# Nine mix products held to the end of the first aggregation, and the small gate matmuls of the last strips placed anew

## What is computed

```python
xn = layernorm(x)
h  = spmm(edges, xn)                                  # first aggregation, A^T applied to xn
S0 = softmax(spmm(edges, h)  @ W0.T + b0)             # first graph layer
S1 = softmax(spmm(edges, [S0, S0]) @ W1.T + b1)       # second graph layer
x  = x + tanh([S0, S1] + h) + mix(xn)                 # mix: linear attention, (q kv) @ wo.T + bo
x  = x + ffn(layernorm(x))                            # top-1 of 8 experts, capacity 489 tokens each
```

## Time and profile before

| | |
|---|---|
| median of 3 runs | 1162.5 us (1161.41 to 1164.13) |
| the profiled execution, first to last instruction (its span) | 1161.9 us |
| TensorE (PE) matmuls, weight loads | 1097.3 us (94%), 701.6 us (60%) |
| VectorE (DVE) | 737.1 us (63%) |
| ScalarE (ACT) | 314.2 us (27%) |
| GpSimd (POOL) | 168.1 us (14%) |
| chain that ended last, by engine | PE 80%, DVE 9%, SPq 3%, issue 3%, ACT 2% |
| its largest lines | L1542 21%, L1691 20%, L1527 11%, L1791 10%, L1779 9%, L1566 2% |
| granted TensorE clock, mean | 0.976 |

### The profile page before, as it was taken

How to read it: one execution, slowest core, us unless ns; L and a number is a source line. 1 busy time by engine, 2 the same in 40 slices (tenths; PEclk the granted TensorE clock), 3 DMA queues, 4 the chain that set the end, 5 groups by cost and what they waited for, 6 DMA issues and landing times.

```text
span 1161.9 us, 14112 instructions
## 1 busy us (share of the span) xinstructions
PE 1097.3 (94%) x4837; PEld 701.6 (60%) x4837; DVE 737.1 (63%) x1681; ACT 314.2 (27%) x1038; POOL 168.1 (14%) x206
## 2 busy tenths in 40 slices
PE   5879999999999999999998999999998799999995
PEld 3446666666666666667793444644447666666664
DVE  8989989998786877777760111116788435554444
ACT  4667767421211222122210111101112211122220
POOL 1112223301010100000000000000234511111111
PEclk9899989999999999999998999999999799999998
DMA  5110111123323223343318998997995584555520
GB/s 168 18 45 13 46 47 46 46 91 121 133 96 133 114 112 121 126 154 136 131 57 323 325 354 292 343 343 275 308 320 213 155 217 117 118 141 136 141 63 7
DMA packets 78871, 178.52 MB, mean 154 GB/s; under 512 B 33567, under 2 KB 62011, under 8 KB 66639
## 3 DMA queue, kind: packets, MB, share of 16 engines
q1 hardware_dynamic: 67550, 126.16, 34.1%
q10 hardware_dynamic: 7120, 43.34, 9.2%
q0 software_dynamic: 4128, 8.08, 2.0%
HBM read 116.23 MB, written 63.77 MB: 155 GB/s over the span
## 4 chain that ended last, share of the span: by engine, by line
PE 80%; DVE 9%; SPq 3%; issue 3%; ACT 2%; DMA 1%; POOLq 0%; POOL 0%; ACTq 0%; DVEq 0%
PE ps L1542 21%; PE ps L1691 20%; PE ps L1527 11%; PE ps L1791 10%; PE ps L1779 9%; PE ps L1566 2%; SPq L465 2%; PE ps L1509 2%; PE ps L1442 1%; PE ps L1495 1%; DVE W L1022 1%; SPq L463 1%; DVE XT L1357 1%; ACT W L746 1%; PE ps L1516 1%
## 5 line engine op out<-in xcount | busy, mean ns | idle before, releaser
L1542 PE MATMUL ps<-RING,XX 128*128 128x512 f32 (+2 forms) x700 | 291.8, 542 | 1.0 <-DVE W L1082 1.0
L1691 PE MATMUL ps<-RING,RY 128*128 128x512 f32 (+4 forms) x750 | 273.7, 523 | 5.8 <-issue 5.8
L1691 PEld LDWEIGHTS ps<-RING,RY 128*128 128x128 f32 x750 | 136.8, 196 | 126.4 <-issue 119.0
L1527 PEld LDWEIGHTS ps<-RING 128*128 128x128 f32 x1250 | 164.5, 193 | 40.8 <-issue 34.1
L774 ACT COPY RING<-ps 128x512 f32<-128x512 f32 (+3 forms) x163 | 91.2, 560 | 312.2 <-PE ps L1527 298.2
L1527 PE MATMUL ps<-RING 128*128 128x128 f32 (+1 forms) x1250 | 171.3, 277 | 0.1
L1542 PEld LDWEIGHTS ps<-RING,XX 128*128 128x128 f32 x700 | 118.5, 191 | 68.8 <-issue 60.7
L1073 DVE TENSOR_TENSOR RING<-iota_n,RY 128x512 f32<-128x512 f32 (+1 forms) x138 | 91.2, 661 | 34.5 <-PE ps L1527 31.8
L1074 DVE TENSOR_TENSOR RING<-iota_n,RY 128x512 f32<-128x512 f32 (+1 forms) x138 | 100.5, 728 | 0.0
L1076 DVE TENSOR_TENSOR RING<-RING,RY 128x512 f32<-128x512 f32 (+1 forms) x138 | 91.1, 660 | 0.0
L900 ACT ACTIVATE RY<-ps,b1T 128x489 f32<-128x489 f32 x64 | 42.9, 670 | 172.2 <-PE ps L1779 172.2
(11 more groups left out here) (258 smaller groups left out, 1295.3 us busy)
## 6 DMA issues: line engine op xcount, KB each, us to landing
RING<-adj_dram SPq DMA_DIRECT2D x60, 1280.0 KB, 6.9
adj_dram<-RING ACTq DMA_DIRECT2D x30, 1280.0 KB, 4.5
rbuf_dram<-W SPq DMA_DIRECT2D x8, 516.0 KB, 5.4
RING<-rbuf_dram SPq DMA_DIRECT2D x8, 516.0 KB, 4.0
xbuf_dram<-W SPq DMA_DIRECT2D x8, 512.0 KB, 3.3
XT<-in_L_ffn_w SPq DMA_DIRECT2D x16, 256.0 KB, 5.1
XT<-in_L_ffn_w SPq DMA_DIRECT2D x4, 1024.0 KB, 8.4
RING<-in_L_ffn_w SPq DMA_DIRECT2D x16, 256.0 KB, 4.9
```

The costliest lines, as they stand in the source:

```text
L1527: last = nc.tensor.matmul(o[:, c:c + w], h[:, 0, i, :], h[:, 1, i, 0:w], start=True, stop=(j != s))
L1542: last = nc.tensor.matmul(ps[:, ACC + dd, 0:w], XN[:, j, dd * H:(dd + 1) * H], at[:, i * w:(i + 1) * w], start=(j == 0), stop=True, skip_g ...
L1691: last = nc.tensor.matmul(o, (Y if l == 0 else S0)[:, j, :], RING[:, slot_of[g % 5], i * across + first:i * across + first + w], start=(j ...
```

## The change

Two separate edits.

**Mix products.** `MIX_AT` ends at tile 15 (iteration 100). Tiles 16 to 24 (`HELD = 16`) come after the loop: 16 and 17 around `hidden_node(23)`, as 22 and 23 did before, and 18 to 24 behind `hidden_node(24)`, ahead of `more_rounds`. They have places of their own in five banks (`HELD_AT`), so none of them waits for a `mixed`; VectorE does the nine `mixed` in a row behind both `hn_out`, each bank's only once all of that bank's products are done. `turns(0, 0)` and `turns(0, 1)`, which use banks 2 and 7, wait for `s_mrd`.

**Last strips.** Strip `kb` keeps `turns(1, ka)` and `logits(ka - 1)` as inserts. `counts(ka - 1)` and `gate_turn(ka)` move from its steps 14 and 22 to steps 4 and 6 of strip `kc`; there `turns(1, kb)` and `logits(ka)` move from steps 4 and 5 to step 13. `counts(ka)` and `gate_turn(kb)` move from step 21 of strip `kc` to behind `turns(1, kc)`. ScalarE does `zout(1, kc)` ahead of `exp8(ka)` and `xtout(kb)`, not behind them.

```diff
--- before.py
+++ after.py
@@ -119,7 +119,8 @@
 for _t in range(NT - 2):
     _k, _i = _t // 4, _t % 4
     HN_AT[NT * _k + 30 + (5 * _i if _k < 5 else _i)] = _t
-MIX_AT = {40 + 4 * _m: _m for _m in range(NT - 3)}
+HELD = 16
+MIX_AT = {40 + 4 * _m: _m for _m in range(HELD)}
 KV_AT, T1_AT, M_AT, FOUND_AT = 33, 37, 39, 60
 
 
@@ -311,7 +312,14 @@
         HNB = 5
         MIXB = 6
         TURN = (2, 7)
-        mix_bank = lambda m: MIXB if m < NT - 2 else ACC + m - (NT - 2)
+        HELD_AT = ((MIXB, 0), (MIXB, D), (KVACC, 0), (KVACC, D), (PROD, 0), (PROD, D), (ACC, 0), (ACC, D), (ACC + 1, 0))
+
+        def mix_out(m):
+            bank, at = HELD_AT[max(m - HELD, 0)]
+            return ps[:, bank, at:at + D]
+
+        def mixes_to_bank(m):
+            return m + 1 if m < HELD else max(n for n in range(HELD, NT) if HELD_AT[n - HELD][0] == HELD_AT[m - HELD][0]) + 1
         XTB = 3
         LGB = 5
         CNB = 6
@@ -879,9 +887,9 @@
             zout(1, kb)
             ex(1, kb)
             tanh(1, kb)
+            zout(1, kc)
             exp8(ka)
             xtout(kb)
-            zout(1, kc)
             ex(1, kc)
             tanh(1, kc)
             xtout(kc)
@@ -1087,9 +1095,9 @@
                 v.tensor_copy(Y[:, t, :], ps[:, HNB, D:D + H]).then_inc(s_hrd, 1)
 
             def mixed(m):
-                dve.wait_ge(s_mixp, m + 1)
+                dve.wait_ge(s_mixp, mixes_to_bank(m))
                 dve.wait_ge(s_bo, m + 1)
-                v.tensor_tensor(X1[:, m, :], X1[:, m, :], ps[:, mix_bank(m), 0:D], ALU.add).then_inc(s_mrd, 1)
+                v.tensor_tensor(X1[:, m, :], X1[:, m, :], mix_out(m), ALU.add).then_inc(s_mrd, 1)
 
             heads = lambda x: x.rearrange("p (h d) -> p h d", d=HD)
             g_v = gvb[:, 0, :].unsqueeze(1).to_broadcast([P, 2, HD])
@@ -1190,11 +1198,10 @@
                 if it - 3 in MIX_AT:
                     mixed(MIX_AT[it - 3])
             strip_out(NS - 1)
-            mixed(NT - 3)
             hn_out(NT - 2)
-            mixed(NT - 2)
             hn_out(NT - 1)
-            mixed(NT - 1)
+            for m in range(HELD, NT):
+                mixed(m)
 
 
             with more_rounds(dve):
@@ -1560,10 +1567,9 @@
 
             def mix(m):
                 pe.wait_ge(s_mv, 1)
-                if m < NT - 2:
-                    ge(pe, s_mrd, m)
+                ge(pe, s_mrd, min(m, HELD))
                 for c in range(2):
-                    last = nc.tensor.matmul(ps[:, mix_bank(m), 0:D], XT[:, c, m * P:(m + 1) * P], M[:, c, :], start=(c == 0), stop=(c == 1))
+                    last = nc.tensor.matmul(mix_out(m), XT[:, c, m * P:(m + 1) * P], M[:, c, :], start=(c == 0), stop=(c == 1))
                 last.then_inc(s_mixp, 1)
 
             turn(0)
@@ -1612,11 +1618,12 @@
                     hidden_node(HN_AT[it])
                 if it in MIX_AT:
                     mix(MIX_AT[it])
-            mix(NT - 3)
+            mix(HELD)
             hidden_node(NT - 2)
-            mix(NT - 2)
+            mix(HELD + 1)
             hidden_node(NT - 1)
-            mix(NT - 1)
+            for m in range(HELD + 2, NT):
+                mix(m)
 
 
             with more_rounds(pe):
@@ -1698,6 +1705,8 @@
             def turns(l, k):
                 b = k % 2
                 pe.wait_ge(s_zev[l], k + 1)
+                if l == 0 and k < 2:
+                    pe.wait_ge(s_mrd, NT)
                 if k >= 2:
                     pe.wait_ge(s_ex[0] if l == 0 else s_nm[1], k - 1)
                 elif l == 1:
@@ -1760,9 +1769,11 @@
                     inserts[23] = [later(gate_turn, k - 1)]
                 strip(1, k, inserts)
             strip(1, ka, {1: [later(logits, ka - 2)], 3: [later(turns, 1, ka - 1)], 15: [later(counts, ka - 2)], 21: [later(gate_turn, ka - 1)]})
-            strip(1, kb, {3: [later(turns, 1, ka)], 4: [later(logits, ka - 1)], 14: [later(counts, ka - 1)], 22: [later(gate_turn, ka)]})
-            strip(1, kc, {4: [later(turns, 1, kb)], 5: [later(logits, ka)], 21: [later(counts, ka), later(gate_turn, kb)]})
+            strip(1, kb, {3: [later(turns, 1, ka)], 4: [later(logits, ka - 1)]})
+            strip(1, kc, {4: [later(counts, ka - 1)], 6: [later(gate_turn, ka)], 13: [later(turns, 1, kb), later(logits, ka)]})
             turns(1, kc)
+            counts(ka)
+            gate_turn(kb)
             logits(kb)
             gate_turn(kc)
             logits(kc)
```

## The result

The median falls from 1162.53 us to 1154.67 (four runs, 1152.17 to 1155.24): -7.9 us by the medians. The ratio over all runs is 0.9926, with a 95% interval of 0.9912 to 0.994; that is -8.6 us, between -10.2 and -7.0. The forecast was 1154.8. Its sum was right, but its term for the clock was not. The two profiles' spans, 1161.9 and 1153.1 us, hide this, since 2.7 us of difference lie ahead of both edits.

The account below looks back on a forecast made before the run. The prediction took TensorE to bound the loop, and VectorE to set the pace in the last strips once the wait goes. Terms -5.2 + 2.5 - 5.0 = -7.7 us, from 1162.5 to 1154.8 us; range 1149.0 to 1159.0.

Parts of the forecast that it names:

- term for the clock: First strip behind the branch: after a 3.1 us idle gap the clock falls as before, no gain; 2.8 us if not.
- the prediction's own last sentence: Wrong if branch time depends more on traffic, the clock stays up, or the queue is deeper than 18 passes.
- Loop: First aggregation's loop, bound by TensorE: six mix products leave it, 0.86 us each, full 5.2 us gained.
- Tail: Loop end to first strip: sequencer lead of 18 passes, branch of 6.0 us, so first strip 2.5 us later.
- The lower bound of 3.1 us: TensorE's branch behind the held products: its shortest time, if it ends when the DMA transfers do.
- The rival of the deep queue: Loop end: all 34 passes fit in TensorE's queue, branch hidden, clock stays up; 1149.7 us, chance 0.10.
- The rival of the short gap: Loop end: branch 4.5 to 5.5 us, gap 1.7 to 2.7, clock stays up; 1151.0 us, chance 0.28.
- Last strips: Strips kb and kc: without the 3.80 us wait, VectorE sets the pace and `biased(kc)` starts 5.0 us earlier.
- edit 2: The last strips' reordering of inserts: forecast gain 5.0 us, bounds 3.3 and 5.8.
- The half gain: Loop bound partly by VectorE's order or stores, or branch fetch 3 to 6 us longer; 1157.4 to 1161.2, chance 0.11.
- the late chunk: Strip kc's first chunk lands late, TensorE stands still and its clock falls; slower, 1164.0 at 14 us, chance 0.03.
- edit 2's moved wait: Last strips: VectorE's order holds `biased(kc)` another 1.7 us or more; 1156.5 to 1158, chance 0.05.

Follow-up runs that it names:

- the first profile: Kernel before, unchanged, profile on which the forecast was built: span 1161.9 us, kernel's median 1162.53 us.
- the other two: Two more profiles of the unchanged kernel before: single times 1164.14 and 1162.86 us.
- held5: Changed kernel with five mix products held (20 to 24), not nine: 1157.68 us, 0.9948 to the kernel before.
- no_branch: Changed kernel without TensorE's fallback and the branch over it: 1150.43 us, 0.9888 to the kernel before.
- after: The changed kernel itself, first profile: median 1154.67 us, 0.9926 to the kernel before.
- before_2: Second profile of the kernel before, nothing changed: single time 1164.14 us.
- after_again: The changed kernel timed and profiled once more, nothing further changed: 1155.03 us, 0.9926 to the kernel before.
- after_3: Third profile of the changed kernel, nothing further changed: single time 1154.77 us.
- vec_order: Changed kernel with VectorE doing `biased(kc)` ahead of `slotted(ka)` and `moments(kb)`: 1152.60 us, 0.9913 to the kernel before.
- both: Changed kernel with `biased(kc)` ahead of `slotted(ka)` and `moments(kb)`, and TensorE's branch register loaded ahead of the held products: 1152.21 us, 0.9905.
- mix_only: Kernel before with only the mix products held: 1159.24 us, 0.9959 to the kernel before.
- stall_back: Changed kernel with `counts(ka - 1)` put back to step 14 of strip `kb`: 1159.32 us, 0.997 to the kernel before.
- gates_only: Kernel before with only the last strips' edit: 1158.72 us, 0.9961 to the kernel before.

## Why the prediction was right

The time came out as forecast, and so did three of the four terms. The step that failed is the fall of the clock; by the prediction's own last sentence a clock that stays up is a sign that it is wrong.

**Loop.** -5.2 forecast, -5.18 in every profile with nine held.

**Tail.** The forecast said +2.5 us, from a lead of 18 passes and a branch of 6.0. The lead: the register load was forecast at 615.4 in the time of the kernel before, and found at 612.8 + 2.48 = 615.3 (the held products start 609.91 - 607.43 = 2.48 us earlier). The branch took 5.5 to 5.7 us with nine held, below the 6.0. The result is +2.1 against the first profile, whose own branch was long, and +2.7 against the other two. `held5` shows that the lead is what limits (twelve passes behind the last `hidden_node` do not hold up the register load, twenty-eight do), and `no_branch` that it is the branch which costs.

The lower bound of 3.1 us, for a branch beside less traffic, lay far off. In `after` the DMA share is 0.63 and 0.64 in the branch's last two full microseconds, in `before_2` it stays at 0.95 or more there, and the branches took 5.64 and 5.78 us. No experiment changed the traffic alone. The rival of the deep queue falls: the sequencer ran no further ahead than some 18 passes, at 256 columns as at 512. The Trainium skill (Advanced Engine Details and Errata, "Engine Queue Depths") gives TensorE 64 entries; no run here shows how many entries a pass takes.

**Clock.** This step failed: "3.1 is nearer to the first, so I take the fall as before, and no gain." The gap was 2.6 to 2.8 us, and with it the clock stayed up in four profiles (`after`, `after_again`, `after_3`, `vec_order`; in `both` too, with 2.1 us) and fell in two (`mix_only`, `stall_back`). What decides between the two, the runs do not show. Nor is the price of a fall one number: it is 1.6 to 1.7 us where the fall lasts 3.4 us, and 2.7 to 2.9 where it lasts 6.8, as in the first profile and `gates_only`. So this term is -1.6 to -2.9 when the clock stays up, and the forecast put it at nothing. The rival of the short gap had the clock right, and its gap of 1.7 to 2.7 us and branch of 4.5 to 5.5 us came about true at their upper ends; its 1151.0 was too low, as it took 1.5 us for the tail and 2.8 for the clock.

**Last strips.** -5.0 forecast, -5.3 against the first profile, -4.4 against the other two, where the lower clock behind the wait was shorter. The order of events came as forecast, VectorE as the pace included: `biased(kc)` starts right behind `slotted(ka)`, and `vec_order` gets 1.35 us by moving it. `stall_back` shows that there is no gain while the wait stands.

**Sum.** The profiles give -8.5 against `before_2` and `before_3` and -9.0 by the means, the medians -7.9, the ratio -8.6. The forecast's -7.7 leaves out a clock term of about -1.6; against `before_2` and `before_3` its edit 2 is 0.6 too large, and that cancels a part. That it meets the median to 0.2 us is thus in part luck. The half gain, the late chunk and edit 2's moved wait did not come. What the clock does in unprofiled runs can't be seen, so the few tenths between these sums stay open; all of them lie inside the interval.

## What to carry to other kernels

Work held back to cover a branch hides it only as far as the sequencer runs ahead of the engine: find that lead in the trace, at a wait that the sequencer passes before the engine reaches the work behind it, and count no more than it. Of a wait on the engine that is the bound, ask which other engine's chain ends next; here 3.8 us of waiting were worth 4.4 to 5.3 us, and the next 1.35 lay in VectorE's order. A sum made from one profile inherits that execution's clock falls: two more profiles of the unchanged kernel would have shown how far the clock and branch terms spread.

## What the runs showed of the hardware

The branch over the skipped code took 5.5 to 6.6 us in twelve profiles. TensorE's sequencer was some 18 passes ahead of the engine, whether a pass took 0.22 us (18.6 passes, the changed kernel) or 0.43. The same idle gap of 2.6 to 2.8 us was followed by 1.2 GHz in two profiles and not in four. A fall there cost 1.6 to 1.7 us, or 2.7 to 2.9 where the lower clock lasted longer. The stretch up to mix(0), which no edit touches, takes 265.7 to 269.3 us, so up to 3.6 us more in one execution than in another.
